# First halves of two column groups of an output projection, run ahead of the unit that feeds their second halves

## What is computed

```python
def step(h, xs):                       # 16 states for each of 1024 channels
    dt_t, B_t, C_t, u_t = xs
    dA = jnp.exp(dt_t[:, :, None] * A)
    h = dA * h + dt_t[:, :, None] * B_t[:, None, :] * u_t[:, :, None]
    return h, jnp.einsum('bdn,bn->bd', h, C_t)
y = scan(step) + u * D
x1 = x + (y * silu(z)) @ w_out.T       # the output projection, 1024 -> 512
x1 + swiglu(rmsnorm(x1) * w)           # feed-forward, 1408 wide
```

## Time and profile before

| | us |
|---|---|
| median of 3 runs (lowest, highest) | 3117.69 (3115.7, 3120.54) |
| the profiled execution, its own time | 3119.29 |
| its span | 3117.5 |
| TensorE, VectorE, ScalarE, GpSimd busy | 2547.0, 2407.6, 1242.0, 1052.8 |
| granted TensorE clock, mean | 0.881 |

### The profile page before, as it was taken

How to read it: one execution, slowest core, us unless ns; L and a number is a source line. 1 busy time by engine, 2 the same in 40 slices (tenths; PEclk the granted TensorE clock), 3 DMA queues, 4 the chain that set the end, 5 groups by cost and what they waited for, 6 DMA issues and landing times.

```text
span 3117.5 us, 21149 instructions
## 1 busy us (share of the span) xinstructions
PE 2547.0 (82%) x6708; PEld 1211.8 (39%) x6708; DVE 2407.6 (77%) x1788; ACT 1242.0 (40%) x1993; POOL 1052.8 (34%) x299
## 2 busy tenths in 40 slices
PE   4787989888969887799698776896987869979965
PEld 1234434333434443344344433443443434445532
DVE  5997898988979988899899989898999883121122
ACT  4334456444353452543534534535335332021231
POOL 1233343344434445424334464244443540000000
PEclk7776999888989998789889997898889879989986
DMA  3124426332212674031126650221266502217810
GB/s 131 29 73 166 137 103 193 103 106 95 64 37 87 216 234 139 26 107 58 38 94 209 220 153 22 94 65 41 75 215 194 155 7 88 71 67 239 284 40 14
DMA packets 160392, 350.13 MB, mean 112 GB/s; under 512 B 30681, under 2 KB 48089, under 8 KB 155609
## 3 DMA queue, kind: packets, MB, share of 16 engines
q1 hardware_dynamic: 134680, 271.89, 28.3%
q10 hardware_dynamic: 20480, 60.10, 5.1%
q0 software_dynamic: 5120, 16.78, 1.6%
HBM read 304.55 MB, written 61.73 MB: 117 GB/s over the span
## 4 chain that ended last, share of the span: by engine, by line
PE 41%; DVE 31%; issue 12%; ACT 8%; POOL 4%; DMA 3%; ACTq 0%; DVEq 0%; SPq 0%; POOLq 0%
DVE hb L1611 13%; PE ps L961 6%; PE ps L968 6%; DVE hb L1619 4%; DVE hb L1524 4%; PE ps L816 4%; PE ps L769 3%; POOL ya L1884 3%; PE ps L823 2%; PE ps L934 2%; PE ps L1004 2%; DMA ring<-in_w_edn 2%; PE ps L1116 2%; PE ps L891 1%; ACT T L1410 1%
## 5 line engine op out<-in xcount | busy, mean ns | idle before, releaser
L1884 POOL TENSOR_TENSOR ya<-ya,hb 128x2048 f32<-128x2048 f32 x188 | 856.7, 4557 | 1334.2 <-DVE hb L1611 1251.1
L1611 DVE TENSOR_TENSOR_SCAN hb<-da,hb 128x2048 f32<-128x2048 f32 x192 | 856.3, 4460 | 2.0 <-ACT da L1158 0.7
L1158 ACT ACTIVATE da<-dl,pk 128x511 f32<-128x511 f32 x768 | 489.3, 711 | 401.1 <-DVE hb L1611 391.0
L1524 DVE TENSOR_TENSOR hb<-du,ps 128x2048 f32<-128x2048 f32 x192 | 436.1, 2271 | 33.8 <-POOL ya L1884 26.1
L1619 DVE TENSOR_TENSOR hb<-hb,ps 128x2048 f32<-128x2048 f32 x192 | 437.6, 2279 | 3.7 <-PE ps L908 2.9
L816 PE MATMUL ps<-V,ring 128*128 128x512 f32 x512 | 245.4, 633 | 20.9 <-DVE V L1552 12.0
L769 PE MATMUL ps<-ring,hid 128*128 128x512 f32 x544 | 247.4, 611 | 3.7 <-DVE hid L1656 3.7
L985 PE MATMUL ps<-ring,hid 128*128 128x352 f32 x480 | 198.1, 496 | 22.2 <-ACT hid L1381 16.2
L989 PE MATMUL ps<-ring,hid 128*128 128x352 f32 x480 | 193.6, 486 | 11.6 <-ACT X L1398 11.5
L1004 PE MATMUL ps<-ring,X 128*128 128x512 f32 x360 | 180.7, 637 | 15.3 <-DMA ring<-in_w_edn 14.5
L961 PE MATMUL ps<-T,ring 128*128 128x512 f32 x352 | 168.7, 624 | 17.5 <-DVE T L1644 17.5
(11 more groups left out here) (283 smaller groups left out, 3457.4 us busy)
## 6 DMA issues: line engine op xcount, KB each, us to landing
ring<-egu SPq DMA_DIRECT2D x240, 352.0 KB, 3.9
ring<-in_w_edn SPq DMA_DIRECT2D x72, 512.0 KB, 5.2
ring<-in_w_fgu SPq DMA_DIRECT2D x44, 512.0 KB, 3.6
hid<-xrows SPq DMA_DIRECT2D x60, 256.0 KB, 4.2
yrows<-X ACTq DMA_DIRECT2D x60, 256.0 KB, 4.7
ring<-wc SPq DMA_DIRECT2D x24, 512.0 KB, 4.3
ring<-in_w_egu SPq DMA_DIRECT2D x24, 512.0 KB, 3.5
ring<-in_w_edn SPq DMA_DIRECT2D x60, 192.0 KB, 4.4
```

Source lines behind the costliest of these rows:

```text
L1158: i = act.activation(dav(n % 2)[:, k, 1:], dl[:, k, 1:], ACT.Exp, scale=Aneg[:, (4 * (u % 3 - 1) if u % 3 else UC) + k, m:m + 1])
L1524: dve.tensor_tensor(hbv(m % NHB), du[:, :, :], wide(ps[:, 5, :], 4), ALU.mult).then_inc(s["dbu"], 1)
L1611: dve.tensor_tensor_scan(hb[:, h, :], da[:, b % 2, :], hb[:, h, :], 0.0, ALU.mult, ALU.add)\
L1884: pool.tensor_tensor(sums, ya[:, :, :], hbv(m % NHB), ALU.add).then_inc(s["acc"], 1)
```

## The change

For the first two column groups the first half (nodes 0 and 2) gets rank 40, waits only for unit 3b+1 and comes after `exp_down` of the sequence before; node 2 also waits for the attention rows of that sequence, which use its bank. The order of the nodes is 0, 2, 1, 3, 4, 5, 6, 7. Nodes 0 to 3 load half a slot of weights each, so that a sequence takes six slots for its projection and not four. The factor of `t_rs` gets a semaphore of its own, `rstd_n`, and the other thresholds of `rstd` go down by one.

```diff
-       ... "mm": KC, "x1": KC, ... "rstd": 8, ...
+       ... "mm": KC, "mm_half": 2, "x1": KC, ... "rstd": 7, "rstd_n": 1, ...
@@ plan()
-        for m in range(2 * KC):
-            at = chain(30, ("mix", b, m), [("pe", 3.6)], at, (("fin", 3 * b + 2, 0), "dve"),
+        at = (("exp_down", b - 1, SHARED - 1), "pe") if b else at
+        for m in (0, 2, 1, 3, 4, 5, 6, 7):
+            early = m in (0, 2)
+            at = chain(40 if early else 30, ("mix", b, m), [("pe", 3.6)], at, (("fin", 3 * b + (1 if early else 2), 0), "dve"),
                        (("x1", b, m // 2 - 2), "dve") if m >= 4 else (("x_load", 0, 0), "act") if b == 0 else None,
-                       (("c_bc", b + 1, 0), "dve") if b + 1 < SEQS else None)
+                       (("c_bc", b + 1, 0), "dve") if m == 2 and b + 1 < SEQS else None,
+                       (("att_end", b - 1, TT - 1), "act") if m == 2 and b else None,
+                       (("xmix", b - 1, TT - 1), "pe") if m == 1 and b else None)
@@ lender(): a half is its own user of a slot
+    if t == "mix" and n < 4:
+        return task
@@ loads()
+                elif t == "mix" and i < 4:
+                    n.append((w_out[i // 2][:, i % 2 * 4 * P:(i % 2 + 1) * 4 * P],) +
+                             (of("mm", b, i // 2 + 1) if i % 2 else of("mm_half", b, i // 2 + 1)))
@@ TensorE
                         m, half = divmod(n, 2)
-                        if half == 0:
+                        if half == 0 or m < 2:
                             cur["mix"] = slot()
                         if n == 0:
-                            pe.wait_ge(*of("h_done", b, 2))
+                            pe.wait_ge(*of("h_done", b, 1))
...
+                        elif n == 2:
+                            if b:
+                                pe.wait_ge(*of("att", b - 1, TT))
                             if b + 1 < SEQS:
                                 pe.wait_ge(*of("c_bc", b + 1, 2))
+                        elif n == 1:
+                            pe.wait_ge(*of("h_done", b, 2))
                         elif half == 0 and m >= 2:
                             pe.wait_ge(*of("x1", b, m - 1))
                         for k in range(4 * half, 4 * half + 4):
-                            i = pe.matmul(ps[:, 4 + 2 * (m % 2), :], cur["mix"][:, k * P:(k + 1) * P], yg[:, k, :],
+                            o = (k if m >= 2 else k % 4) * P
+                            i = pe.matmul(ps[:, 4 + 2 * (m % 2), :], cur["mix"][:, o:o + P], yg[:, k, :],
                                           start=(k == 0), stop=(k == UC - 1))
                         if half:
                             i.then_inc(s["mm"], 1)
+                        elif m < 2:
+                            i.then_inc(s["mm_half"], 1)
@@ TensorE at ffn_mm 0, VectorE at t_rs
-                                pe.wait_ge(*of("rstd", b, 1))
+                                pe.wait_ge(*of("rstd_n", b, 1))
-                        dve.wait_ge(*of("rstd", b, 1))
+                        dve.wait_ge(*of("rstd_n", b, 1))
@@ ScalarE
-                    act.activation(dst, dst, ACT.Exp, scale=-0.5).then_inc(s[pre + "rstd"], 1)
+                    act.activation(dst, dst, ACT.Exp, scale=-0.5).then_inc(s["rstd_n" if key == "n" else pre + "rstd"], 1)
```

More of the change, by code:

```diff
@@ L67 @@
        "h_done": 2, "delta": 3, "hx_in": 16, "ctx_in": 16, "tctx_in": 16, "x_in": 16, "xv_in": 16, "out_done": 16 * TT,
-       "mm": KC, "x1": KC, "resid": 1, "xn": KC, "sq": 5, "stat": 1, "rstd": 8, "xe": 16, "bst": 15, "shift": 5, "nrm": 4 * TT,
+       "mm": KC, "mm_half": 2, "x1": KC, "resid": 1, "xn": KC, "sq": 5, "stat": 1, "rstd": 7, "rstd_n": 1, "xe": 16, "bst": 15, "shift": 5, "nrm": 4 * TT,
        "v": 4, "lv": 1, "down": 20, "gt": FA + SHARED, "gu": FA + SHARED, "th": FA + SHARED, "sg": FA + SHARED,
@@ L410 @@
      "dbu", "scan", "hc", "skip", "h_done", "firsts", "acc"] +
-    ["mm", "gt", "gu", "fold", "folded", "down", "stat", "nat", "res_t", "route", "bx", "bg", "bt", "bd", "rank", "qk", "en", "en_t", "score",
+    ["mm", "mm_half", "gt", "gu", "fold", "folded", "down", "stat", "nat", "res_t", "route", "bx", "bg", "bt", "bd", "rank", "qk", "en", "en_t", "score",
      "att_t", "wt_t",
-     "sq", "ln", "rstd", "th", "rexp", "qk_sb", "en_exp", "seg_exp", "att_sb", "fexp", "xs",
+     "sq", "ln", "rstd", "rstd_n", "th", "rexp", "qk_sb", "en_exp", "seg_exp", "att_sb", "fexp", "xs",
      "x1", "xn", "sg", "hid", "xe_b", "bth", "bsg", "bhid", "te_b", "ye_b", "msk", "pos", "eid", "scat", "gath0", "gath1", "cy", "cz",
@@ L1366, in _ @@
                         act.wait_ge(*of("stat", b, 1))
-                        rstd(R[:, :], ps[:, 4, :], "t", 0)
+                        rstd(R[:, :], ps[:, 4, :], "n", 0)
                     elif t in ("ffn_ev", "exp_ev"):
@@ L1403, in _ @@
                         rstd(r4, mv[:, :, 1], "t", 1)
-                        act.wait_ge(*of("rstd", b, (2, 3, 4, 6, 7)[n]))
+                        act.wait_ge(*of("rstd", b, (1, 2, 3, 5, 6)[n]))
                         for e in range(TT):
@@ L1764, in _ @@
                         dve.wait_ge(*of("score", b, 1))
-                        dve.wait_ge(*of("rstd", b, 5))
+                        dve.wait_ge(*of("rstd", b, 4))
                         for e in range(TT):
@@ L1824, in _ @@
                     elif t == "bias_y":
-                        dve.wait_ge(*of("rstd", b, 8))
+                        dve.wait_ge(*of("rstd", b, 7))
                         for e in range(TT):
```

## The result

The changed kernel takes 3135.26 us (median of 4 runs, 3129.46 to 3139.9) where the kernel before took 3117.35 beside it: ratio 1.0057, 95% interval 1.0043 to 1.0071. It is **18 us slower**; 3105 was predicted, and the range ended at 3119.

The account below looks back on a forecast made before the run. Up to 2574 us VectorE's work and standstills bound the kernel, behind it the token chain, mostly on TensorE. -6.9 - 7.4 + 2.1 - 1.0 = -13.2 us from 3119.29, 3106.1; median 1.6 lower, rounded to 3105 us; range 3094 to 3119.

Parts of the forecast that it names:

- rival A: VectorE takes nothing: new small waits replace the two at L1644; 3110.8 to 3112.9 us, chance 0.21.
- Part 5: Sequence 0: a half between unit 3's step-size matmuls delays VectorE; +2.1 us, bounds 0 to +4.2, cold +11 at most.
- Part 1: Sequence 3's projection: two nodes leave the busy stretch and the feed-forward starts sooner, unstopped by the bias layer; -6.9 us.
- Part 2: Halves go into TensorE's idle time behind `exp_down`; a 2.05 us delay of segment attention is covered by the scan.
- Part 3: Loads: two more issues per sequence hide behind `exp_down`; 0 us, uncovered 2.6 to 4.1 us each.
- Part 4: Sequences 1 and 2, wait ahead of L1644: own semaphore saves 3.8 us, earlier L942 3.6; together -7.4 us.
- Part 6: At 2574 us, `fin` of unit 11 and projection start: an earlier token chain gives up to 2.7 us; -1.0 taken.
- Rival B: Slower: uninterruptible halves stand before step sizes or rows VectorE needs, up to 5.5 us each cold; 3133 us with four, chance 0.10.
- C: The clock gains too: L1027 after a filled gap runs in 1.91 instead of 3.67 us; 3101 us, chance 0.10.
- D: Halves land directly before the rest, behind unit 3b+2, or TensorE's list is late by as much; 3114 to 3118 us, chance 0.09.

Follow-up runs that it names:

- e4: Changed code with the lists of the kernel before, halves of sequences 1 to 3 moved, sequence 0 as before: 3115.56 us, 0.9996.
- e10: Lists of the kernel before, only sequence 0's two halves moved to unit 3's step sizes, as in the changed kernel: 3119.95 us, 1.0013.
- e5: Changed kernel, scheduler told that the squares and R's product come behind the bias layer: 3135.33 us.
- e6: Changed kernel without early halves in sequence 0: 3122.41 us, 1.002.
- e7: Placebo: changed code, no half moved, scheduler's constant for the hop between engines 0.16 instead of 0.15 us: 3138.81 us, 1.007.
- e12: Second placebo: changed code, no half moved, scheduler's look ahead 0.42 instead of 0.4 us: 3129.22 us, 1.0035.
- e11: Changed kernel's plan with early halves in sequence 0 alone, the scheduler free to reorder the rest: 3124.55 us, 1.0028.
- e3: Changed code with the lists of the kernel before, edited for sequence 3 alone (halves behind `exp_down`): 3115.92 us, ratio 1.0.
- e8: e3's lists, with R made before the bias layer's factor on ScalarE and used first on VectorE in sequence 3: 3118.32 us, 1.0001.
- e2: Changed code (half loads, banks, counters) with the kernel before's lists on every engine, no half moved: 3110.33 us, 0.9989.
- e9: e8 with three extra matmuls that nobody reads in TensorE's two gaps near the end: 3112.61 us, 0.9985.

## Why the prediction was wrong

**What failed above all is a step that the prediction took without a word:** that the work around the halves stays in its order, or is none the worse for a new one. It said once that "the scheduler will reorder both sides", and priced that at half of 7.3 us, as a gain; rival A let a new order take the gains in front of L1644, never more. Any change of the scheduler's input gives new lists: on TensorE 438 lines of difference. Two placebos move no half and lose 23 and 13 us, the new places in before's order (e4) lose nothing, and one and the same pair of halves costs 3.8 us in the old order and 8.4 in a new one. All five kernels with newly searched lists besides the changed one are slower than before, and the changed kernel lies within their spread. So of the 18 us some 14 are the order, and 3 to 4 are Part 5's. The direct test, the changed kernel's order with the halves put back, was not run. Why six new orders out of six are worse is not shown either; before's order came out of the same search, with constants that may have been chosen because its order was a good one.

**The bill.** In the profiles the changed kernel loses 11.7 us up to the last scan, 3.3 of them by the halves of sequence 0 if they cost there what they cost in e10, and 10.7 more at the last `xmix`. The latter is one place in VectorE's list. In the changed kernel, e5, e6, e7 and e12 the norm ahead of `xmix` of sequence 2 has one scan of the last unit behind it, and `xmix` costs 11.2 to 13.4 us behind `fin`; in the nine others it has two, and 2.3 to 2.9. The scans end there, so nothing hides it. All of what e6 loses is this. That this place alone does it wasn't tested by moving it back, but no profile is on the other side. The two columns together, less the 2.7 us of before, give 22.4, 21.6, 8.9, 25.5, 10.1 and 15.8 us for the six kernels with new lists (after, e5, e6, e7, e11, e12), where the medians say 17.9, 19.6, 6.7, 23.1, 8.4 and 13.1.

What happens further ahead is shown in part. The table has 28 stretches at sequences 1 and 2. In ten the residual sum takes 8.09 to 8.69 us, and these are 62.7 to 72.5 us long; in the other 18 it takes 4.5 us, and they are 59.7 to 61.3. The ten are all in kernels with new lists, and each of those has one or two. The changed kernel at sequence 1 shows what happens; VectorE, then GpSimd:
```profile
1366.14 4.41 DVE L1628 TENSOR_TENSOR_SCAN hb<-da,hb 128x2048 f32<-128x2048 f32 x1
1370.47 2.45 DVE L1828 TENSOR_TENSOR T<-ps,T 128x512 f32<-128x512 f32 x4
1372.96 2.47 DVE L1835 BATCH_NORM_STATS2 sm<-T 128x6 f32<-128x512 f32 x4
...
1375.84 6.05 DVE L1661 SCALAR_TENSOR_TENSOR T<-V,pk,R 128x512 f32<-128x512 f32 x4
```
```profile
1366.30 8.60 POOL L1861 TENSOR_TENSOR X<-X,V 128x2048 f32<-128x2048 f32 x1 [8.84 <-DVE V L1655]
1374.84 4.50 POOL L1901 TENSOR_TENSOR ya<-ya,hb 128x2048 f32<-128x2048 f32 x1
```
This scan began at 1379.97 us before, behind L1644; now it stands ahead. The residual sum starts beside the scan and takes 8.60 us; the scan's own sum, L1901, then falls on L1661, and its four instructions take 6.05 us instead of 2.74. All four sequences of the changed kernel have such a stall (6.18, 6.05, 6.10 and 6.97 us); before, only sequence 0 had one (7.04). This is a marker and one link, not the bill: the scan is work done, and the one behind it starts 77.8 us after the start of unit 5's `fin`, 77.2 before. What is late is the feed-forward. And e6, with both sums long, loses nothing up to the last scan, where e7 loses 17 us. Which swaps cost the changed kernel the other 8 us of its scans stays open.

**Part 1** (-6.9): none came. The failed step is "even a bias layer that gains nothing doesn't stop it". It compared the end of L1818 with the feed-forward, but L1818 isn't the bias layer's last word. Its product L1827 stands ahead of L1644 on VectorE, in the kernel before:
```profile
2614.39 3.70 DVE L1827 TENSOR_SCALAR T<-T,mv,sm 128x512 f32<-128x512 f32 x4 [2.54 <-ACT sm L1152]
2618.30 2.74 DVE L1644 SCALAR_TENSOR_TENSOR T<-V,pk,R 128x512 f32<-128x512 f32 x4 [0.22 <-ACT R L1152]
```
A bias layer that gains nothing holds L1644 until 2618.1 us, 0.2 us before it starts anyway. And the bias layer gains little, because its matmuls stand in TensorE's queue ahead of the squares, and they wait for VectorE's routing. What can go is only the node and the gap between these two groups, 3.44 + 0.79, and with the filler 4.5 us did go. Without it the clock took it back in two profiles of three: two groups at low clock cost 5.04 us (e3; e8 the same, e4 not). In the changed kernel it is lost otherwise, by the swapped order and the stall of L1661.
The prediction named the clock for the halves and not for the place that they leave. The Trainium skill (TensorE: Matmul & The Clock Gate, Part 1), which it cited, says that activity releases the full rate. The two runs with and without filler agree with that: 6.05 and 6.38 us without, 3.70 and 3.70 with. But e4 ran in 3.70 and 3.70 us without it.

**Part 2** (hidden): right where placed by hand (e4), and the sites were the forecast ones. **Part 3** (0): right, e2. **Part 4** (-7.4): the wait did shrink by 1.84 us twice, but the gain was given back in L1644's own duration and in VectorE's fixed work; 0.9998. That VectorE's bound lets nothing through was rival A, and it holds: with before's lists, every gain of the token chain ahead of 2574 us vanished by the next unit. **Part 5** (+2.1, bounds 0 and 4.2, cold up to 11): 3.3 in the profile, 3.8 in the medians, for two halves and not one. **Part 6** (-1.0): the wrong sign; it took the token chain to come earlier, and `xmix` came 13.6 us behind `fin` instead of 2.9.

**Rival B**, the slower one, had a wrong mechanism and, by luck, nearly the right time (3133): cold halves in front of the step sizes exist at sequence 0 and cost 3.3 us, not 22; in sequences 1 and 2 they cost nothing. **C** is refuted in the changed kernel: the L1044 behind its gap of 7.86 us at sequence 1 is as slow as L1027 before (3.68 and 3.67 us). What the clock did, it did the other way round. **D** is out: the halves stand where they should, 1226.92 us at sequence 1 and not behind unit 5. Of the signs named ahead, the feed-forward 38.3 us behind its projection (45.4) and the 498 us behind it (503.6) failed; `fin` of unit 11 at 2575.6 us was a sign of A.

## What to carry to other kernels

Where lists come from a search, price the search first: change a constant of it by a hair, time that, and take its spread (here 13 and 23 us) as the noise floor of every such edit; or freeze the lists and edit them by hand. Then look where two kinds of work end together, as scans and token chain do here: one place in a list cost 10.7 us there, while the new order of e6 cost nothing as long as there were scans to do. Before counting removed matmuls as a gain, look at what the next ones in the queue wait for, and whether they would then start behind gaps at low clock. If they do, a few idle matmuls in the gap are worth a try.

## What the runs showed of the hardware

- With 16 records of 0.43 us taken out of a stretch without gaps there were two gaps of 1.77 and 1.37 us, and in two profiles (e3, e8) the 16 records behind them took 12.4 us instead of 7.4, at a clock of 0.87. In a third (e4), with the same list on TensorE for this stretch, they took 7.4, at 0.98. With six records of filler, 2.9 us in all, they took 7.4 as well (e9). A single profile doesn't settle what such gaps do.
- VectorE's product L1644 takes 2.74 us for four instructions alone, 7.04 when it begins with GpSimd's 4.5 us sum (sequence 0, 750.59 and 750.61 us), and 6.05 when it begins 1.0 us behind it: the first of the four lasts about until GpSimd's is done (5.05 us at 750.59). GpSimd's sum takes 8.6 instead of 4.5 us when it begins beside a scan.
- Profiles of kernels whose lists are the same there differ by up to 9.5 us at the first scan of unit 1 (291.3 to 300.9 us), and take 495.0 to 503.3 us for the part behind the last feed-forward's start. Stages were therefore compared within one profile.
